# A transformer block on one core: the slot of projections moved between the scores and the values' products

## What is computed

```python
def _attn(x, ctx, Wq, Wk, Wv, Wo, bo):          # 16 heads of 64
    q, k, v = x @ Wq, ctx @ Wk, ctx @ Wv        # each split into heads
    sim = jnp.einsum('bihd,bjhd->bhij', q, k) * 64 ** -0.5
    attn = jax.nn.softmax(sim, axis=-1)
    out = jnp.einsum('bhij,bjhd->bihd', attn, v).reshape(b, n, INNER)
    return out @ Wo + bo
h = _ln(x, g1, be1)
x = _attn(h, h, Wq1, Wk1, Wv1, Wo1, bo1) + x
h = _ln(x, g2, be2)
x = _attn(h, context, Wq2, Wk2, Wv2, Wo2, bo2) + x
h = _ln(x, g3, be3)
y = h @ Wp + bp
a, gate = y[..., :1024], y[..., 1024:]
x = a * jax.nn.gelu(gate, approximate=False) @ W2 + b2 + x
```

## Time and profile before

| what | us |
|---|---|
| median of 3 runs (lowest, highest) | 2042.43 (2042.31, 2042.63) |
| the profiled execution | 2042.06 |
| its span, from the first to the last instruction | 2040.3 |
| PE busy | 2028.6 |
| GpSimd busy | 1416.4 |
| VectorE busy | 1385.3 |
| ScalarE busy | 1159.7 |
| the loop of 64 steps, from 63.9 to about 1512 | 1448 |

### The profile page before, as it was taken

How to read it: one execution, slowest core, us unless ns; L and a number is a source line. 1 busy time by engine, 2 the same in 40 slices (tenths; PEclk the granted TensorE clock), 3 DMA queues, 4 the chain that set the end, 5 groups by cost and what they waited for, 6 DMA issues and landing times.

```text
span 2040.3 us, 31825 instructions
## 1 busy us (share of the span) xinstructions
PE 2028.6 (99%) x12500; PEld 1387.7 (68%) x12500; DVE 1385.3 (68%) x2124; ACT 1159.7 (57%) x1851; POOL 1416.4 (69%) x745
## 2 busy tenths in 40 slices
PE   8999999999999999999999999999999999999999
PEld 7665665666565566665655666566558999888888
DVE  6477677666767785578678566757777898754453
ACT  5566577544557675255667544657665666533332
POOL 2699799975979998679799867979895576300000
PEclk9999999999999999999999999999999999999999
DMA  7300000001000000010000001000010530000100
GB/s 229 124 7 21 6 7 16 6 6 47 17 11 6 16 6 6 1 63 6 6 6 22 6 1 52 6 6 1 22 47 16 145 84 1 1 21 22 42 11 31
DMA packets 46566, 58.74 MB, mean 29 GB/s; under 512 B 5969, under 2 KB 40401, under 8 KB 45265
## 3 DMA queue, kind: packets, MB, share of 16 engines
q1 hardware_dynamic: 46416, 56.71, 8.9%
HBM read 38.88 MB, written 17.83 MB: 28 GB/s over the span
## 4 chain that ended last, share of the span: by engine, by line
PE 99%; ACT 1%; DVE 0%; DMA 0%; issue 0%; SPq 0%; ACTq 0%
PE score L494 22%; PE score L477 18%; PE score L603 9%; PE score L481 6%; PE score L425 5%; PE attn_project L617 4%; PE attn_project L589 4%; PE score L559 4%; PE attn_project L425 4%; PE first_score L451 4%; PE attn_project L528 3%; PE score L437 3%; PE score L528 2%; PE attn_project L451 2%; PE first_score L518 2%; PE attn_project L437 1%
## 5 line engine op out<-in xcount | busy, mean ns | idle before, releaser
L1316 POOL TENSOR_TENSOR acc<-acc,pT 128x1024 f32<-128x1024 f32 x384 | 914.6, 2382 | 55.4 <-POOL acc L1316 0.9
L1100 ACT ACTIVATE pT<-score 128x1024 f32<-128x1024 f32 x512 | 525.7, 1027 | 102.8 <-PE score L481 59.1
L477 PE MATMUL score<-qk 64*128 64x512 f32 x3072 | 456.2, 399 | 1.5 <-ACT oT L1111 0.9
L494 PE MATMUL score<-pT,vT 128*64 128x512 f32 x2016 | 446.5, 595 | 0.0
L780 DVE TENSOR_REDUCE nmax<-first_score 128x1 f32<-128x512 f32 x512 | 347.9, 679 | 3.5 <-PE first_score L451 1.4
L780 DVE TENSOR_REDUCE nmax<-attn_project 128x1 f32<-128x512 f32 x512 | 347.1, 678 | 0.0
L477 PEld LDWEIGHTS score<-qk 64*128 64x128 f32 x3072 | 257.1, 184 | 120.7 <-ACT pT L1100 67.9
L494 PEld LDWEIGHTS score<-pT,vT 128*64 128x64 f32 x2016 | 139.1, 137 | 289.4 <-issue 251.8
L1313 POOL TENSOR_TENSOR acc<-pT 128x1024 f32<-128x1024 f32 x64 | 154.0, 2406 | 150.3 <-ACT pT L1100 150.3
L802 DVE RECIPROCAL sums<-sums 128x512 f32<-128x512 f32 (+1 forms) x65 | 214.4, 3299 | 57.5 <-ACT sums L1125 56.9
L481 PE MATMUL score<-shift,pick 64*128 64x512 f32 x1024 | 205.5, 391 | 0.0
(11 more groups left out here) (160 smaller groups left out, 3056.1 us busy)
## 6 DMA issues: line engine op xcount, KB each, us to landing
xres<-x_middle SPq DMA_DIRECT2D x10, 512.0 KB, 3.7
xres<-in_x SPq DMA_DIRECT2D x4, 1024.0 KB, 7.6
raw_qk<-in_L_xattn_Wq SPq DMA_DIRECT2D x32, 128.0 KB, 2.2
raw_qk<-in_L_xattn_Wk SPq DMA_DIRECT2D x32, 128.0 KB, 2.4
raw_v<-in_L_xattn_Wv SPq DMA_DIRECT2D x8, 512.0 KB, 4.1
keys_all<-keys SPq DMA_DIRECT2D x1, 4096.0 KB, 12.1
values_all<-values SPq DMA_DIRECT2D x1, 4096.0 KB, 12.4
out_x<-xres SPq DMA_DIRECT2D x7, 512.0 KB, 2.9
```

What stands on the lines that cost most here:

```text
L477: e.matmul(bank, qk[P % 2][r, 2 + h, keys], qk[P % 2][r, w, queries], start=(part == 0), stop=False)
L494: last = e.matmul(banks[bank][head * DH:(head + 1) * DH, :], vT[:, v_slot(D, jt), c0:c0 + DH], pT[:, jt, head, :], start=(jt == 0), stop=( ...
L1100: e.activation(pT[:, jt].rearrange("p h n -> p (h n)"), SC[R % 2][:, :], ACT.Exp).then_inc(s.exponential, 1)
L1316: e.tensor_tensor(total, total, pT[:, jt], ALU.add).then_inc(s.probs_added, 1)
```

## The change

The slot is cut in two. `slot(C)` keeps the two projections, the turn of the maxima (now between the two) and the output projection, and comes between the scores and the products (on PE ahead of the sums, on ScalarE right behind the exponentials, on VectorE ahead of the inversion). `late_slot(C)` has the norm's halves and the values, and stays behind the products. The banks change: projections go through PV and S0a, the norm's halves through PJ and T1, the products through S1a. The two first-pass matmuls of a round stand ahead of that round's scores instead of behind them. `scale_oT` moves from GpSimd to VectorE, behind the inversion of the same sums.

```diff
             P, c = divmod(C, CHUNKS)
+            b, n = divmod(C, BC)
+            after = P + 1 + c
+            if after >= B * PAIRS:
+                return []
+            jobs = [("qk", after, 1 - c, "PV"), ("max", C + 1, "T1"), ("qk", after, 3 - c, "S0a")]
+            if b and n in (1, 2):
+                jobs += [("out1", b - 1, TPC * (n - 1) + t, ("T0", "S0b", "S1b")[t % 3]) for t in range(TPC)]
+            return jobs
+
+        def late_slot(C):
+
+            P, c = divmod(C, CHUNKS)
             (b, n), D = divmod(C, BC), C // (4 * CHUNKS)
-            jobs = [("max", C + 1, "T1")] if C + 1 < NC else []
-            between = []
+            jobs = []
             if n - BC + 4 in range(CHUNKS if b + 1 < B else 1):
-                between += [("ln", next_norm(b, n - BC + 4), k) for k in range(KT)]
-            if b and n in (1, 2):
-                between += [("out1", b - 1, TPC * (n - 1) + t) for t in range(TPC)]
+                jobs += [("ln", next_norm(b, n - BC + 4), k, ("PJ", "T1")[k]) for k in range(KT)]
             if C % (4 * CHUNKS) == 4 * CHUNKS - 1 and D + 1 < GROUPS:
-                between += [("v", D + 1, jt) for jt in range(TILES)]
...
+                jobs += [("v", D + 1, jt, ("S0b", "T1", "PJ")[jt % 3]) for jt in range(TILES)]
+            if P + 1 + c >= B * PAIRS and C + 1 < NC:
+                jobs += [("max", C + 1, "T1")]
             return jobs
...
-                bank = "S0a" if C + 1 < NC else "PV"
+                bank = "S1a" if C + 1 < NC else "PV"
...
                 for jt in range(TILES):
+                    if C + 1 < NC:
+                        for head in range(2):
+                            first_score(*next_part(C + 1, jt), head)
                     for part in range(len(TERMS) + 1):
                         for head in range(2):
                             score(TILES * C + jt, part, head)
-                    if C + 1 < NC:
-                        for head in range(2):
-                            first_score(*next_part(C + 1, jt), head)
+                whole_array(slot(C))
...
                 for jt in range(TILES):
                     attend(TILES * C + jt)
-                whole_array(slot(C))
+                whole_array(late_slot(C))
...
+            def scale_oT(C):
+                there = oT[:, C // CHUNKS % PRING, C % CHUNKS * BANK:(C % CHUNKS + 1) * BANK]
+                need.wait_ge(s.sum_inverse, 2 * (C + 1))
+                need.wait_ge(s.oT_written, C + 1)
+                e.tensor_tensor(there, there, sums[:, C % 2, :], ALU.mult).then_inc(s.oT_scaled, 1)
...
                     gather_max(C + 1)
+                whole_array(slot(C))
...
                 if C >= 2:
                     invert_sums(C - 2)
+                    scale_oT(C - 2)
...
-                if C >= 3:
-                    scale_oT(C - 3)
```

More of the change, by code:

```diff
@@ L943, in _ @@
                     invert_sums(C - 1)
-                whole_array(slot(C))
+                    scale_oT(C - 1)
+                whole_array(late_slot(C))
             for i in range(NT + 3):
@@ L959, in _ @@
                     invert_sums(NC - 1, (i - 1,))
+                if i == 2:
+                    scale_oT(NC - 1)
                 if i in (TPC + 1, 2 * TPC + 1):
@@ L1110, in write_oT @@
                     need.wait_ge(s.out1_product, TILES * b + TPC * (c + 1))
-                e.copy(oT[:, P % PRING, c * BANK:(c + 1) * BANK], banks["S0a" if C + 1 < NC else "PV"]).then_inc(s.oT_written, 1)
+                e.copy(oT[:, P % PRING, c * BANK:(c + 1) * BANK], banks["S1a" if C + 1 < NC else "PV"]).then_inc(s.oT_written, 1)
             def copy_sums(C, bank="PJ"):
@@ L1316, in add_probs @@
                     e.tensor_tensor(total, total, pT[:, jt], ALU.add).then_inc(s.probs_added, 1)
[L1318 to L1322, removed]
             def scale2(i):
```

4 lines of the change are left out of this document (removed).

## The result

| | us |
|---|---|
| before, median of 4 runs (lowest, highest) | 2042.37 (2042.07, 2042.63) |
| after, median of 4 runs (lowest, highest) | 2084.70 (2083.89, 2086.59) |
| ratio (95% interval) | 1.0209 (1.0191 to 1.0226) |
| the profiled execution of after; its span | 2084.22; 2082.4 |

The account below looks back on a forecast made before the run. PE was taken as the bound, busy 99% with hardly a gap. Changes of kind +6, halves +16.5, scaling +10 and products' bank -0.8 gave 31.7 us on 2042.06: 2074 us, 1.6% slower, range 2050 to 2096.

Parts of the forecast that it names:

- PE's changes of kind: PE at the slot ahead of the products: +0.06 us in 61 steps, 0.18 more in fourteen; +6 us, ends -6 to +12.
- a sign of being wrong: PE waiting in the slot itself, for gathered maxima or a bank: counted at nothing; 0.1 us there would be 6 us.
- The halves: Norm's halves last in the step: PE waits 2.35 us before the second round's first-pass pair, seven steps; +16.5 us (14 to 20).
- The scaling: Outputs scaled on VectorE at 2.1 us each: even steps with statistics or means' sign come late; +10 us (0 to 26).
- an ordinary even step loses nothing: VectorE comes 0.45 us late for the next first-pass maximum, and PE bears about that much.
- The upper end of this term: Scalings of 2.9 us: eleven ordinary steps lose 0.8 us, six 1.9 and four 1.55; 26 us.
- The products' bank: Products in S1a instead of S0a: two steps near the end start without waiting for the copy; -0.8 us.
- (a): Rival: scaling on VectorE meets no GpSimd work, so its term is 0; 2064 us, chance 0.17.
- (c): Rival: rounds get shorter, the moved first-pass pair covering 67.9 us of weight-load waits for ScalarE; 2006 us, chance 0.06.
- (d): Rival: the halves' waits do not come about and scaling meets no GpSimd work; 2047 us, chance 0.07.
- (b): Rival: scaling waits longest each time, since VectorE and GpSimd run in step with PE; 2090 us, chance 0.13.

## Why the prediction came out 10 us short

**PE's changes of kind: right a step; a wait for a bank was left out.** The 22 steps that have nothing special lost 0.06 us each, as forecast, and the seven with v 0.23, where 0.24 was forecast. The lines of step 35 show the pieces: 3.11 us for the slot, and 0.33 from a step's first first-pass pair to its scores (916.14 to 916.47), where a pair within a block takes 0.23. The nine steps at the output projection lost 3.2 us and not 0.5: 1.8 is the sums' wait for bank T0, 0.7 belongs to the scaling (n = 0, below). A wait of PE in the slot for a bank was the one thing that I had counted at nothing, and named as a sign of being wrong; it came, in three steps. And bank PV would have come 0.35 us late in every step, had the first pass stayed behind: I argued with the turn alone and did not ask it of the banks, so that PV was free was luck.

**The halves: right in place, count and size; one thing was not in the sum.** All engines behind step 12, answering:

```profile
341.86 0.66 PE L342 MATMUL attn_project<-ident,xn 128*128 128x128 f32 x4
...
343.37 0.82 DVE L742 TENSOR_SCALAR attn_project<-attn_project,cols 128x512 f32<-128x512 f32 x1 [0.38 <-ACT hT L1058]
...
343.92 0.40 PE L486 MATMUL score<-shift,pick 64*128 64x512 f32 x2
...
345.67 0.69 DVE L747 TENSOR_TENSOR hT<-first_score,hT 128x512 fp32r<-128x512 f32 x1
...
346.51 0.47 PE L456 MATMUL first_score<-qk 64*128 64x512 f32 x1 [2.20 <-DVE hT L747]
```

PE stands from 344.3 to 346.5, 2.20 us where 2.35 was worked out. Five of the six steps in the table's row are 2.45 to 2.6 us longer than before, which has some 0.2 us for the change of kind in it; the sixth lost 3.8, because PE's clock fell behind the wait (last section). All seven make 19.0 us, of which 15.2 is the wait and 1.3 the clock.

**The scaling: mechanism right, the term mis-sized, 16 for 10.** The choice of 2.1 us a scaling was made by the row that was nearest to it; what decides it is when it starts. Of the 64 scalings of after, all 52 that started beside an addition with more than 0.15 us to go ended 0.55 us after that addition's end. In an even step the start is fixed by the sums' copies, and in 24 of the 32 even steps the time is nearly the same, 2.1 to 2.3 us. VectorE, GpSimd and PE, from step 6 into step 7:

```profile
201.21 3.35 DVE L808 RECIPROCAL sums<-sums 128x512 f32<-128x512 f32 x1 [2.14 <-ACT sums L1142]
...
204.01 2.36 POOL L1334 TENSOR_TENSOR acc<-acc,pT 128x1024 f32<-128x1024 f32 x1
...
204.60 2.32 DVE L814 TENSOR_TENSOR oT<-oT,sums 128x512 f32<-128x512 f32 x1
...
205.65 0.50 PE L456 MATMUL first_score<-qk 64*128 64x512 f32 x1
...
207.92 0.67 DVE L786 TENSOR_REDUCE nmax<-first_score 128x1 f32<-128x512 f32 x1
...
208.64 0.50 PE L456 MATMUL first_score<-qk 64*128 64x512 f32 x1 [0.41 <-DVE nmax L786]
...
209.24 0.49 PE L456 MATMUL attn_project<-qk 64*128 64x512 f32 x1
```

The addition ends at 206.37, the scaling at 206.92. The Trainium skill, page "SBUF — State Buffer", section "Who interferes with whom", says that a VectorE instruction with two inputs in SBUF and a GpSimd instruction that reads SBUF contend for ports that they share, and that these are an exclusive lock. The traces agree: the scaling ends 0.55 us behind the addition's end, and takes 1160 ns in the mean with additions half as long.

What made the term larger is that VectorE is later than I reckoned, by 0.3 us in each of these steps. The inversion starts 4.44 us ahead of the next first-pass pair (201.21 to 205.65), as forecast, but takes 3.39 us to the start of the scaling, where the prediction wrote 3.25 although shows 3.35; and the scaling takes 2.32 and not 2.1. So VectorE is free 0.77 us behind the moment at which the first maximum could be taken (206.92 against 206.15), and not 0.45. PE bears 0.46 of that, as I had it, and the rest is lost. With two statistics that gives 1.3 us and 1.3 to 1.4 were lost, where the forecast had 1.1; with the means, whose sign took 0.90 us here, it gives 1.1 and 1.2 were lost in three batches, where it had 0.75. PE's lines show how the loss comes about: its first wait is only 0.41 us, but that is one head, and the bank of the other head comes 0.6 us later (208.64 and 209.24, the time of one maximum). That an ordinary even step loses nothing, with a margin of 0.01 us, held only where the scaling takes 2.1 us or less: in the last three batches n = 0 and n = 4, and in the last batch n = 6 and 8, lost 0.2 to 0.35 us each. Not foreseen were also the shift of step 63, for which PE waits 0.95 us behind a scaling, and 0.7 us behind the loop: 12.8 + 1.0 (n = 4) + 0.7 (n = 0) + 1.0 + 0.7 = 16.2. (The upper end of this term counts eleven ordinary steps and doesn't say which; the loop has 21 even steps from step 2 on without statistics or means.)

**The products' bank: wrong sign.** I asked what S1a does for steps 62 and 63, and not who uses S1a last. Step 61 has no slot any more, and its products, PE in order of time, wait for the last exponential, just as all odd steps do with the bank alone changed:

```profile
1510.23 7.09 PE L499 MATMUL score<-pT,vT 128*64 128x512 f32 x32 [1.11 <-ACT pT L1117]
```

Forecast -0.8. With the scaling on GpSimd steps 62 and 63 do come 0.2 and 0.3 us sooner, but the wait in step 61 costs 1.1.

The sum read back: 2.9 changes of kind, 2.5 at the output projection (1.8 of it bank T0), 19.0 halves (1.3 of it the clock), 16.2 scaling, 0.6 bank, 0.9 ahead of the loop in code that the change doesn't touch (its start differs by up to 1.2 us between the profiles here). The scaling's 6 us too little are most of the 10 that are missing. The rivals (a), (c) and (d) are out; (b), a scaling that waits long each time because engines run in step, describes most of the even steps, but at 2.2 to 2.3 us and not 2.9.

## What to carry to other kernels

When a block is moved, ask of every piece left behind it what it now stands in front of: here seven pairs of turned halves lost the projections that had covered them, came to stand directly before the consumer of their banks, and cost 19 us, where the moved projections themselves cost 0.06 us a step. Ask the same of every bank that a moved piece writes last: the next writer may have come closer. Price an instruction that shares a port with a neighbour by the neighbour's remaining time at the moment it starts, not by a mean; and where a margin is as thin as 0.01 us, as that of the ordinary even steps was, let the forecast carry what 0.3 us more would cost. Parts of a change are not additive: two that cost 30 us each alone cost next to nothing in the ordinary steps together with a third, and to have PV free, another bank for the first projection was cheaper than another place for the first pass.

## What the runs showed of the hardware

**A clock that falls after some waits.** Behind step 13 of after, 2 us stretches of the trace (length, busy time and count of PE, PEld, DVE, ACT, POOL; then the granted clock, DMA share, GB/s):

```profile
366.00:368.00 2.00, 1.52 (x12) 0.88 (x10) 0.57 (x1) 1.97 (x4) 1.92 (x3) 1.00 0.00 0
368.00:370.00 2.00, 0.34 (x2) 0.34 (x4) 1.97 (x4) 0.94 (x2) 2.00 (x3) 0.89 0.02 6
370.00:372.00 2.00, 2.00 (x12) 1.51 (x12) 1.99 (x4) 0.00 (x0) 1.58 (x3) 0.50 0.42 125
372.00:374.00 2.00, 2.00 (x16) 1.65 (x14) 1.29 (x2) 1.20 (x2) 0.67 (x1) 0.75 0.00 0
374.00:376.00 2.00, 2.00 (x20) 1.45 (x18) 1.98 (x4) 1.88 (x2) 1.86 (x2) 1.00 0.03 8
```

PE had stood for 2.13 us and was at the lower of its two levels, 1.2 GHz (the 0.50 of the third line), for about 3 us afterwards, which cost 1.3 us more than the other waits of the same length. It is not every time: in the four profiles with such waits (2.1 to 2.2 us of PE idle) the matmuls behind them were slow in 1 of 7 places (after), 3 of 7 (scaling back on GpSimd), 1 of 3 (n = 12 in the slot) and 2 of 7 (additions in halves); behind the 21 waits of about 1.2 us in the three kernels with the first pass behind, in none. Why one wait is followed by it and the next, as long, is not, stays open.

**Small instructions are held too.** The 128x8 instruction above ended 0.02 to 0.04 us after GpSimd's instruction in flight in every place that had one beside it, in the four profiles I read for it. It takes 0.10 us by itself and 2.25 us there: its size says nothing of its time. The same section of the page "SBUF — State Buffer" of the Trainium skill counts this form (a tensor with a constant) among those that can contend with GpSimd, where its operands meet certain conditions. These rows agree.
